# Two graph-attention layers on one core: another order of calls in the edge loop, a written order for its last steps, and no phase between the layers

## The chip, the core and the metric

The kernel runs on one core of a Trainium2 chip. Its engines work side by side and wait for each other through semaphores: PE (TensorE) multiplies and transposes, ACT (ScalarE) evaluates functions and copies, DVE (VectorE) works element by element, POOL (GpSimd) issues the indirect gathers, SP (SyncE) issues the plain DMAs. The metric is the device time of one execution in microseconds, as the median of the runs. Profiles come from one profiled execution; durations in this document are read from it.

## The reference

`x` has 3125 nodes of 128 features; 100,000 edges are given as `src` and `dst`, sorted by `dst`. Two layers (`DEPTH = 2`) with two heads each are computed, and the sum with the input is normalised:

```python
for i in range(DEPTH):
    h = _layer_norm(x, ln1_g[i], ln1_b[i])
    g = _gatv2(h, src, dst, Wl[i], bl[i], Wr[i], br[i], att[i], gat_b[i])
    x = x + (g @ proj_W[i] + proj_b[i])
    h = _layer_norm(x, ln2_g[i], ln2_b[i])
    x = x + (jax.nn.gelu(h @ W1[i] + b1[i]) @ W2[i] + b2[i])
# _gatv2: xl = h @ Wl + bl, xr = h @ Wr + br
#   score = einsum(leaky_relu(xl[src] + xr[dst]), att); alpha = segment softmax of score over dst
#   out = segment_sum(xl[src] * alpha, dst) + gat_b
# after the layers: x = _layernorm(x_in + x)
```

## The kernel before

**Tables.** A first phase (`setup`) builds index tables; a second (`project_nodes`) writes `xl` of layer 0 and its scores' linear part to a table in HBM, 130 numbers per node and head, and `xr` split into three bf16 parts. Between the layers stands one more phase, `begin_layer`, which copies the starting tables back (`reset_state` on POOL, `reset_tables` and `make_dests` on DVE).

**Edge loop.** The 100,000 edges are cut into 391 units of 256. A step handles two units, so there are 196 steps (`NO`), the last with one unit. Each unit takes two indirect gathers of 128 rows on POOL (L969, tile `rows`), 782 per layer. POOL may run ten steps ahead of the sums (`sums_ready`, L966). For step i the engines do:

- PE `project(u)` (L1091, L1094): transposes the gathered rows into PSUM and adds `xr`; ACT `relu` (L1209) reads it into `lz`.
- PE `score(i-1)` (L1066, L1071, L1077); ACT `keep_scores` (L1230) copies the scores out; DVE `lowest` (L1363 to L1382) finds each window's running extreme, one step after another, since `nm` is carried on; ACT `exponent` (L1222) makes the weights `ex`.
- PE `turn(i-4)` (L1143) transposes the weights, ACT `weigh` (L1215) copies them to `wgt`, PE `total(i-5)` (L1160) sums the rows by them, DVE `accumulate` (L1454) adds into `acc`.
- DVE `one_hot` (L1351) prepares the next step's masks, ACT `linear` (L1237) its linear part.

**Nodes.** When a tile of 128 nodes has all its edges, about every eighth step, it is carried through the rest of the layer, spread over some 20 steps by `nodes(i, at)`: ACT `stg` (L1303, L1306), PE L1109, DVE division (L1473), PE L1118, ACT `gT`, PE L1123, DVE `x1` and its moments, ACT square root, DVE `xn2`, PE L1168, ACT `h2`, PE L1129, ACT gelu (L1290), PE L1176, DVE `x2`, and in layer 0 the next layer's projection (L1135), split into three parts (L1507, L1563) and stored by SP (L1029, L1033, L1038); in layer 1 the normalised output (L1534, L1023). The last five tiles, 20 to 24, are called T0 to T4 here; T3 and T4 can only begin when the last steps' sums are in.

**What sets the order.** Every engine's program is written out by Python loops over i; nothing reorders it. In the loop of before PE calls `turn(i - 4)` first in a step, ahead of the projections (L1180 to L1190), and ACT calls `weigh` and `exponent` ahead of `keep_scores` and `linear` (L1316 to L1328). From step 195 another fixed order holds to the end (L1191, L1329), and after the last sums DVE also brings the tables of window positions on (`next_pass`, `next_tables`, L1389 to L1429).

## Time and profile before

| | us |
|---|---|
| median of 3 runs (lowest, highest) | 2196.34 (2195.72, 2197.27) |
| the profiled execution | 2195.76 |
| its span, first to last instruction | 2194.1 |
| gathers of layer 0, first start to last end | 92.68 to 1076.88 |
| gathers of layer 1, first start to last end | 1149.34 to 2131.37 |

The span is 1.66 us shorter than the profiled execution's own time, and that is 0.58 us below the median. Of the engines' busy shares PE has 78%, POOL 70%, ACT 67% and DVE 56%. These are averages over two long loops and the stretches behind them; which engine sets the pace has to be read from the waits. Idle time marked "issue" is time in which an engine waited for nothing that the profile shows.

### The profile page before, as it was taken

Reading aid. Unit: us, or ns where it says so; the run is one execution under the profiler, and the core shown is the slowest. Engines: PE = TensorE matmul, PEld = TensorE weight load, DVE = VectorE, ACT = ScalarE, POOL = GpSimd, SP = SyncE. Lnnn points to the kernel's source line nnn. Section 1 sums busy time; section 2 is a strip of 40 time slices with the busy share of each in tenths; the row PEclk is TensorE's granted clock in tenths of the full one; section 3 lists DMA queues with packets and bytes.
Section 4 is the critical chain, followed back from the end, with each engine's and each line's share of the span. In section 5 each row is a group of like instructions: output and inputs, shape, how many; then the busy total and the mean of one; then the engine's idle time right before and its main releaser. Section 6 shows DMA issues by size and latency. Waiting matters only on the chain. (4 is left out here: it accounts for less than half of the span.)

```text
span 2194.1 us, 67356 instructions
## 1 busy us (share of the span) xinstructions
PE 1706.7 (78%) x19783; PEld 1308.7 (60%) x19783; DVE 1233.8 (56%) x5168; ACT 1462.3 (67%) x3260; POOL 1541.2 (70%) x1664
## 2 busy tenths in 40 slices
PE   2677887888888888888846778888887888778885
PEld 1355666666666666666534556666666666666664
DVE  7545565556565565556553455554655555555554
ACT  4455777777777777677634567677777776677674
POOL 3777777777777777777407777777777777777760
PEclk6888998999999999999977988998999899999896
DMA  4655556666666666665316556556556565565540
GB/s 114 202 157 152 158 162 165 168 161 170 162 165 165 162 171 165 161 169 164 100 37 171 153 148 167 158 154 164 156 155 165 153 166 160 149 167 158 151 132 9
DMA packets 236751, 332.74 MB, mean 152 GB/s; under 512 B 51010, under 2 KB 160490, under 8 KB 236394
## 3 DMA queue, kind: packets, MB, share of 16 engines
q0 software_dynamic: 75072, 208.30, 36.8%
q1 hardware_dynamic: 161322, 120.16, 18.5%
q8 instruction: 165, 2.70, 0.5%
q14 instruction: 192, 1.57, 0.2%
HBM read 308.02 MB, written 20.25 MB: 150 GB/s over the span
## 5 line engine op out<-in xcount | busy, mean ns | idle before, releaser
L969 POOL DMA_INDIRECT rows<-table,src_t x1564 | 1490.3, 953 | 483.7 <-issue 468.3
L1209 ACT ACTIVATE lz<-psum 128x512 f32<-128x512 f32 x782 | 467.0, 597 | 550.0 <-PE psum L1094 530.0
L1091 PE MATMUL psum<-ident,rows 128*128 128x128 f32 x3128 | 536.3, 299 | 111.5 <-DMA rows<-table,src_t 111.0
L1454 DVE SCALAR_TENSOR_TENSOR acc<-acc,keep,psum 128x129 f32 x782 | 273.0, 349 | 602.1 <-PE psum L1160 348.2
L1091 PEld LDWEIGHTS psum<-ident,rows 128*128 128x128 f32 x3128 | 409.8, 155 | 148.4 <-DMA rows<-table,src_t 139.3
L1143 PE MATMUL psum<-ident,ex 128*128 128x128 f32 x784 | 175.7, 308 | 292.6 <-ACT ex L1222 289.6
L1094 PE MATMUL psum<-oh,xrw 96*128 96x256 bf16 x1564 | 332.9, 297 | 0.0
L1143 PEld LDWEIGHTS psum<-ident,ex 128*128 128x128 f32 x784 | 87.3, 147 | 379.2 <-ACT ex L1222 347.7
L1160 PE MATMUL psum<-rows,wgt 128*32 128x129 f32 x6256 | 255.7, 285 | 5.3 <-DVE acc L1454 4.7
L1077 PE MATMUL psum<-lz,att_w 128*32 128x256 f32 x3128 | 257.2, 407 | 0.0
L1364 DVE TENSOR_REDUCE low<-hold_s 128x1 f32<-128x256 f32 x392 | 161.9, 413 | 164.1 <-ACT hold_s L1230 162.6
L1160 PEld LDWEIGHTS psum<-rows,wgt 128*32 128x32 f32 x6256 | 186.2, 116 | 103.2 <-issue 35.7
L1222 ACT ACTIVATE ex<-hold_s,peak 128x256 f32<-128x256 f32 x392 | 201.9, 515 | 66.7 <-DVE peak L1382 63.2
L1351 DVE TENSOR_SCALAR oh<-relb,win_col,less 128x256 bf16<-128x256 int16 x782 | 234.9, 344 | 11.1 <-DMA relb<-cyc_d 10.9
L1094 PEld LDWEIGHTS psum<-oh,xrw 96*128 96x128 bf16 x1564 | 167.9, 107 | 15.9
L1066 PE MATMUL psum<-ident,lin 128*128 128x128 f32 (+1 forms) x784 | 164.6, 294 | 0.0
L1237 ACT COPY lin<-rows 128x256 f32<-128x256 f32 x392 | 161.9, 413 | 0.0
L1230 ACT COPY hold_s<-psum 128x256 f32<-128x256 f32 x392 | 142.6, 364 | 17.5 <-PE psum L1077 17.1
L1215 ACT COPY wgt<-psum 128x256 f32<-128x256 f32 x392 | 143.6, 366 | 0.9 <-PE psum L1143 0.9
L1109 PE MATMUL psum<-stg,sel 128*64 128x129 f32 x1200 | 117.9, 291 | 4.3 <-ACT stg L1306 4.3
L1071 PE MATMUL psum<-oh,mask_w 128*32 128x256 bf16 x1564 | 120.6, 298 | 0.0
L1222 ACT ACT_TABLE_LOAD x90 | 115.5, 1283 | 1.6
(245 smaller groups left out, 1970.3 us busy)
## 6 DMA issues: line engine op xcount, KB each, us to landing
xrw<-xr_split SPq DMA_DIRECT2D x782, 48.0 KB
relb<-rel_d SPq DMA_DIRECT2D x194, 192.0 KB
rows<-table,src_t POOLq DMA_INDIRECT x1564
relb<-cyc_d SPq DMA_DIRECT2D x194, 64.0 KB
xr_split<-split SPq DMA_DIRECT2D x50, 192.0 KB, 1.9
table<-row SPq DMA_DIRECT2D x50, 130.0 KB, 2.1
x_mid<-x SPq DMA_DIRECT2D x25, 64.0 KB
xo<-x_mid SPq DMA_DIRECT2D x25, 64.0 KB
```

The lines of the kernel that those rows point to most:

```text
L969: pool.indirect_dma_start(rows[:, ring(u), t, u % M, :, :].rearrange("p h c -> p (h c)"), None, s["tables"][layer][0:NP, :], bass.Indirect ...
L1066: pe.matmul(out[0:n, t * P:t * P + P], lin[:, g % 2, t, 0:n], s["ident"][:, :], is_transpose=True, start=(t == 0), stop=False, skip_group_ ...
L1077: m = pe.matmul(out[o:o + W, 0:UE], w["att_w"][:, h * W:h * W + W], lz[:, u % (2 * M), h * UE:h * UE + UE], start=False, stop=True, skip_g ...
L1091: pe.matmul(z[:, o:o + P], rows[:, ring(u), t, u % M, h, 0:D], s["ident"][:, :], is_transpose=True, start=(h == 0 and t == 0), stop=False, ...
L1094: m = pe.matmul(z[:, h * UE:h * UE + UE], xrw[:, place(u), h * D:h * D + D], oh[0:3 * W, u % (3 * M), :], start=False, stop=(h == H - 1), ...
L1143: m = pe.transpose(ps[4][:, t * P:t * P + P], ex[:, g % 2, t * P:t * P + P], s["ident"][:, :])
L1160: m = pe.matmul(sum_bank(g)[o:o + W, c:c + D + 1], wgt[:, g % 2, t, q:q + W], rows[:, ring(u), t, u % M, h, 0:D + 1], start=True, stop=True)
L1209: act.activation(lz[:, u % (2 * M), :], ps[u % M][:, :], ACT.Relu).then_inc(lz_ready, 1)
L1222: act.activation(ex[0:n, g % 2, :], hold_s[0:n, c, :], ACT.Exp, bias=peak[0:n, c:c + 1], scale=-1.0).then_inc(ex_ready, 1)
L1237: act.copy(lin[:, g % 2, :, :].rearrange("p t (c w) -> p (t c) w", w=W), rows[:, ring(g * M), :, :, :, D + 1:RC].rearrange("p t u h c -> p ...
L1351: m = v.tensor_scalar(oh[:, u % (3 * M), :], relb[:, u % RING, :], s["win_col"][:, 0:1], s["less"][:, 0:1], ALU.is_equal, ALU.subtract)
L1454: m = v.scalar_tensor_tensor(a, a, s["keep"][:, u:u + 1], sum_bank(g)[:, c:c + D + 1], ALU.mult, ALU.add)
```

## The change

**Edge loop.** On PE `turn(i - 4)` moves behind `project` and `score`, ahead of `total(i - 5)`. On ACT `keep_scores` and `linear` come ahead of `weigh` and `exponent`. The loops end at step 190 (`DRAIN = NO - 6`); DVE loads some slot numbers earlier so that the last steps need no loads.

**Last steps.** From there on each engine has a written list of calls. In it T3 and T4 have buffers of their own (`slot`, four each for `x2`, `xn1`, `row`, `xrf`, `rest`, `split`), T2 to T4 have a second PSUM bank (`alt`), the next projection is cut into a right and a left half, and SP loads the stores' places before it waits for data.

**Layers.** `begin_layer` is gone. The tables are brought on, or set back at a layer's end, by POOL behind its last gather (`next_places`, `restart_places`, `next_window`, `restart_window`, `next_tables`), and POOL takes three each of the additions `xob` and `x1b` for T2 to T4. The places of both layers' stores are prepared in `project_nodes` (one `make_dests` more on DVE).

The diff, cut to its core (the functions named in the lists hold the same instructions as before unless said above):

```diff
         for layer in range(L):
-            if layer > 0:
-                scratch(begin_layer, st, layer)
             with nc.Fori(0, n_pass) as _:
                 scratch(edge_pass, wts, st, layer)
...
-def begin_layer(nc, sb, sem, ps, s, layer):
-
-    state = sem("state")
-    moved = sem("moved")
-    with nc.Block() as block:
-        @block.gpsimd
-        def _(pool):
...
+    def next_places(pool):
+
+        link(pool, pool.tensor_scalar(s["count"][:, :], s["count"][:, :], 1.0, None, ALU.add))
+        link(pool, pool.tensor_tensor(hop[:, :], s["at_s"][:, :], s["at_a"][:, :], ALU.subtract))
+        link(pool, pool.tensor_tensor(hop[:, :], hop[:, :], s["at_a"][:, :], ALU.subtract))
+        link(pool, pool.tensor_scalar(hop[:, :], hop[:, :], float(TRASH), s["gen"][0:1, :], ALU.add, ALU.mult))
+        link(pool, pool.tensor_tensor(s["at_a"][:, :], s["at_a"][:, :], hop[:, :], ALU.add))
...
+    def restart_places(pool):
+
+        link(pool, pool.tensor_scalar(over[:, :], s["gen"][:, :], -8.0 * NT, s["count"][:, 0:1], ALU.mult, ALU.add))
+        link(pool, pool.tensor_scalar(over[:, :], over[:, :], 0.5, None, ALU.is_ge))
...
+    T0, T1, T2, T3, T4 = range(NT - 5, NT)
+    DRAIN = NO - 6
+    assert node_step(T0) + 16 == node_step(T1) + 8 == node_step(T2) == DRAIN + 4 and (NU - 3) % RELS == 0
...
+            bias_residual(T2)
+            next_places(pool)
+            bias_residual(T3)
+            if not last:
+                restart_places(pool)
+            bias_residual(T4)
+            pool.wait_ge(added, NO)
+            next_window(pool)
+            if not last:
+                restart_window(pool)
+            bias_middle(T2)
+            next_tables(pool)
+            bias_middle(T3)
+            bias_middle(T4)
+            pool.wait_ge(staged, NT)
+            link(pool, pool.tensor_copy(s["tab_s"][:, :], tf[:, :]))
+            if not last:
+                link(pool, pool.tensor_scalar(s["acc"][:, 0, :], s["acc"][:, 0, :], on[:, 0:1], None, ALU.mult))
+            tables_moved = make_dests(pool, s, layer, moved, moves[0])
+            pool.wait_ge(listed, 1)
+            set_dests(pool, s, layer, moved, tables_moved)
+
...
+                        store_split(t, place_of(t))
+            rels(NU - 3)
+            ranges(NO - 4)
+            if last:
+                store_out(T0, places_of(T0))
+            ranges(NO - 3)
+            old_rows(T2)
+            if not last:
+                store_row(T0, place_of(T0))
+            ranges(NO - 2)
+            ranges(NO - 1)
...
+                store_split(T0, place_of(T0))
+                old_rows(T3)
+                to1, to2, to3, to4 = [place_of(t) for t in (T1, T2, T3, T4)]
+                sp.sem_inc(listed)
+                store_middle(T1, to1)
+                old_rows(T4)
+                store_middle(T2, to2)
+                store_middle(T3, to3)
+                store_middle(T4, to4)
+                store_row(T1, to1)
+                store_row(T2, to2)
+                store_row(T3, to3)
+                store_split(T1, to1)
+                store_split(T2, to2)
+                store_row(T4, to4)
+                store_split(T3, to3)
+                store_split(T4, to4)
...
-            for i in range(NO - 1):
-                if of_step(i - 4):
-                    turn(i - 4)
-                late_work(i)
-                for u in of_step(i):
-                    project(u)
-                if of_step(i - 1):
-                    score(i - 1)
...
+            for i in range(DRAIN):
                 for u in of_step(i):
                     project(u)
                 if of_step(i - 1):
@@ -1197,8 +1384,111 @@
                     turn(i - 4)
                 if of_step(i - 5):
                     total(i - 5)
...
+            score(NO - 7)
+            turn(NO - 10)
...
+            project(NU - 1)
+            score(NO - 2)
+            score(NO - 1)
+            turn(NO - 4)
+            total(NO - 5)
+            total(NO - 4)
+            project_sums(T2)
+            turn(NO - 3)
+            total(NO - 3)
+            turn(NO - 2)
+            total(NO - 2)
+            turn(NO - 1)
+            total(NO - 1)
+            combine(T3, 0)
+            combine(T3, 1)
+            combine(T4, 0)
+            combine(T4, 1)
+            turn_sums(T3)
+            narrow(T1)
+            turn_sums(T4)
+            project_sums(T3)
+            project_sums(T4)
+            turn_second(T2)
+            widen(T2)
+            turn_second(T3)
+            turn_second(T4)
...
+                turn_first(T4)
+                project_right(T4)
+                project_left(T4)
...
-            for i in range(NO - 1):
-                early_nodes(i)
+                    bias_sums(t)
                 for u in of_step(i):
                     relu(u)
-                if of_step(i - 4):
-                    weigh(i - 4)
-                middle_nodes(i)
-                if of_step(i - 3):
-                    exponent(i - 3)
                 if of_step(i - 1):
                     keep_scores(i - 1)
                 linear(i)
-                late_nodes(i)
-            for i in range(NO - 1, END):
-                for u in of_step(i):
-                    relu(u)
-                if of_step(i):
-                    linear(i)
-                if of_step(i - 1):
-                    keep_scores(i - 1)
+                if of_step(i - 4):
+                    weigh(i - 4)
...
+            exponent(NO - 1)
+            weigh(NO - 2)
+            weigh(NO - 1)
+            act.activation(spare[:, 0:1], s["eps_t"][:, 0:1], ACT.Gelu_apprx_tanh)
+            stage(T3, at_T3)
+            stage(T4, at_T4)
+            gelu(T1)
+            act.activation(spare[:, 1:2], s["eps_t"][:, 0:1], ACT.Sqrt)
+            bias_sums(T3)
+            deviation2(T2)
+            bias_sums(T4)
+            deviation1(T1)
+            deviation2(T3)
+            scale_second(T2)
+            deviation2(T4)
+            act.activation(spare[:, 2:3], s["eps_t"][:, 0:1], ACT.Gelu_apprx_tanh)
+            gelu(T2)
+            scale_second(T3)
...
+            gelu(T3)
+            gelu(T4)
+            act.activation(spare[:, 3:4], s["eps_t"][:, 0:1], ACT.Sqrt)
+            deviation1(T2)
...
+            for i in range(DRAIN):
+                accumulate(i - 6)
...
+            accumulate(NO - 7)
+            divide_sums(T2)
+            next_hot(NO - 1)
+            lowest(NO - 4)
+            accumulate(NO - 6)
+            lowest(NO - 3)
+            lowest(NO - 2)
+            accumulate(NO - 5)
+            lowest(NO - 1)
+            accumulate(NO - 4)
+            add_first(T2)
+            accumulate(NO - 3)
+            moments_second(T2)
+            accumulate(NO - 2)
+            accumulate(NO - 1)
+            divide_sums(T3)
+            divide_sums(T4)
+            add_second(T1)
+            moments_first(T1)
...
+                remainder(T4)
+                add_left(T4)
+                third_part(T3)
+                third_part(T4)
```

**PE, a step of layer 0's loop, before:** `ident,rows` and `oh,xrw` are the projections of two units, `ident,lin` to `lz,att_w` the score, `ident,ex` the turn, `rows,wgt` the sum.

```order
L1143 MATMUL psum<-ident,ex 128x128 x2
L1091 MATMUL psum<-ident,rows 128x128 x4
L1094 MATMUL psum<-oh,xrw 128x256 x2
L1091 MATMUL psum<-ident,rows 128x128 x4
L1094 MATMUL psum<-oh,xrw 128x256 x2
L1066 MATMUL psum<-ident,lin 128x128 x2
L1071 MATMUL psum<-oh,mask_w 32x256 x4
L1077 MATMUL psum<-lz,att_w 32x256 x4
L1160 MATMUL psum<-rows,wgt 32x129 x8
```

The same step in the changed kernel:

```order
L1275 MATMUL psum<-ident,rows 128x128 x4
L1278 MATMUL psum<-oh,xrw 128x256 x2
L1275 MATMUL psum<-ident,rows 128x128 x4
L1278 MATMUL psum<-oh,xrw 128x256 x2
L1250 MATMUL psum<-ident,lin 128x128 x2
L1255 MATMUL psum<-oh,mask_w 32x256 x4
L1261 MATMUL psum<-lz,att_w 32x256 x4
L1287 MATMUL psum<-ident,ex 128x128 x2
L1304 MATMUL psum<-rows,wgt 32x129 x8
```

The turn stood first in the step; it now stands eighth, between the score and the sum.

**PE, the last turns and sums of layer 0, before** (`ident,xn`, `h,w` and `wlr,h` are node work of T1 and T0, `stg,sel` the gathering of a tile's sums from the staged windows):

```order
L1143 MATMUL psum<-ident,ex 128x128 x2
L1160 MATMUL psum<-rows,wgt 32x129 x8
L1143 MATMUL psum<-ident,ex 128x128 x2
L1160 MATMUL psum<-rows,wgt 32x129 x8
L1143 MATMUL psum<-ident,ex 128x128 x2
L1160 MATMUL psum<-rows,wgt 32x129 x8
L1168 MATMUL psum<-ident,xn_3 128x128
L1172 MATMUL psum<-ident,xn_3 128x128
L1160 MATMUL psum<-rows,wgt 32x129 x4
L1129 MATMUL psum<-h_3,w_0 128x128 x4
L1135 MATMUL psum<-wlr,h_3 128x512
L1109 MATMUL psum<-stg_3,sel 64x129 x6
```

The same in the changed kernel (`pw,gT` projects T2's sums, `an` are the divided sums of T3 and T4, `w_0,ge` the second half of T1's hidden layer):

```order
L1304 MATMUL psum<-rows,wgt 32x129 x16
L1337 MATMUL psum<-pw,gT_3 128x128 x2
L1287 MATMUL psum<-ident,ex 128x128 x2
L1304 MATMUL psum<-rows,wgt 32x129 x8
L1287 MATMUL psum<-ident,ex 128x128 x2
L1304 MATMUL psum<-rows,wgt 32x129 x8
L1287 MATMUL psum<-ident,ex 128x128 x2
L1304 MATMUL psum<-rows,wgt 32x129 x4
L1319 MATMUL psum<-stg_3,sel 64x129 x24
L1330 MATMUL psum<-ident,an_3 128x128 x2
L1358 MATMUL psum<-w_0,ge_3 128x128 x4
L1330 MATMUL psum<-ident,an_3 128x128 x2
```

Before the last sum (x4) came transposes of T1 and T0, and a hidden layer and a projection stood between it and the first half of T3's gathering (x6). Now that sum follows its turn, and all four halves for T3 and T4 (x24) follow it at once.

**POOL, from the last gathers of layer 0 to those of layer 1, before:**

```order
L969 DMA rows<-table,src_t 128x260 x782
L959 UNCONDITIONAL_BRANCH
L128 ISA
L179 REGISTER_ALU
L179 COMPARE_AND_BRANCH
L732 UNCONDITIONAL_BRANCH
L707 MEMSET step 128x1
L708 MEMSET count 1x1
L709 COPY win_col<-win_col 128x1
L710 COPY at_x<-at_x 1x391
L711 COPY at_s<-at_s 1x391
L712 COPY at_a<-at_a 1x391
```

In the changed kernel POOL goes on behind the gathers, within the same phase (the first 11 of 50 instructions):

```order
L1033 DMA rows<-table,src_t 128x260 x782
L1045 TENSOR_TENSOR xob_3<-xo_3,pb_row 128x128
L964 TENSOR_SCALAR count<-count 128x1
L965 TENSOR_TENSOR hop<-at_s,at_a 1x391
L966 TENSOR_TENSOR hop<-hop,at_a 1x391
L967 TENSOR_SCALAR hop<-hop,gen 1x391
L968 TENSOR_TENSOR at_a<-at_a,hop 1x391
L969 TENSOR_SCALAR at_x<-at_x,step 1x391
L972 TENSOR_SCALAR at_s<-at_s,step 1x391
L973 TENSOR_SCALAR hop<-at_s 1x391
L974 TENSOR_TENSOR at_s<-at_s,hop 1x391
L1045 TENSOR_TENSOR xob_3<-xo_3,pb_row 128x128
```

The copies of a phase of its own became arithmetic on the tables behind the last gather.

## Rows read from the trace of the kernel before

**Rows 1.** The page, part 1: busy time, share of the span, instructions

```profile
PE 1706.7 (78%) x19783; PEld 1308.7 (60%) x19783; DVE 1233.8 (56%) x5168; ACT 1462.3 (67%) x3260; POOL 1541.2 (70%) x1664
```

**Rows 2.** Line 969, POOL's gathers: ns min/median/max; idle before them until

```profile
L969 POOL DMA_INDIRECT rows<-table,src_t x1564: 940/946/1291, 92.7 to 2130.4; - x196
...
  issue: 468.3, 1525
  PE psum L1160: 11.0, 36
```

**Rows 3.** POOL in order of time: start us, us, what, idle before it

```profile
92.68 1.18 POOL L969 DMA_INDIRECT rows<-table,src_t  x1 [3.97 <-issue]
...
1075.94 0.94 POOL L969 DMA_INDIRECT rows<-table,src_t  x1 [0.30 <-issue]
1143.55 0.10 POOL L707 MEMSET step<- 128x1 f32 x1 [66.67 <-SPq L731]
...
1149.34 0.97 POOL L969 DMA_INDIRECT rows<-table,src_t  x1 [3.73 <-POOLq L129]
...
2130.42 0.95 POOL L969 DMA_INDIRECT rows<-table,src_t  x1 [0.30 <-issue]
```

**Rows 4.** PE's waits: us in total, times, longest us

```profile
PE psum L1143 <- ACT ex L1222: 289.6, 171, 3.1
PE psum L1091 <- DMA rows<-table,src_t: 111.0, 70, 17.7
```

**Rows 5.** POOL, then PE, in order of time, about us 2028

```profile
2026.97 0.95 POOL L969 DMA_INDIRECT rows<-table,src_t  x1 [0.30 <-issue]
...
2029.74 0.66 PE L1091 MATMUL psum<-ident,rows 128*128 128x128 f32 x4 [1.02 <-DMA rows<-table,src_t]
```

**Rows 6.** PE in order of time, at the end of layer 0

```profile
1073.00 0.38 PE L1143 MATMUL psum<-ident,ex 128*128 128x128 f32 x2
...
1075.94 1.16 PE L1109 MATMUL psum<-stg,sel 128*64 128x129 f32 x12
1079.92 0.44 PE L1143 MATMUL psum<-ident,ex 128*128 128x128 f32 x2 [2.82 <-ACT ex L1222]
...
1084.90 0.66 PE L1091 MATMUL psum<-ident,rows 128*128 128x128 f32 x4
...
1108.95 4.18 PE L1109 MATMUL psum<-stg,sel 128*64 128x129 f32 x36 [0.58 <-ACT stg L1306]
```

**Rows 7.** The page, part 5: one costly group

```profile
L1209 ACT ACTIVATE lz<-psum 128x512 f32<-128x512 f32 x782 | 467.0, 597 | 550.0 <-PE psum L1094 530.0
```

**Rows 8.** DVE in order of time, at both layers' ends

```profile
1089.28 0.42 DVE L1364 TENSOR_REDUCE low<-hold_s 128x1 f32<-128x256 f32 x1 [0.66 <-ACT hold_s L1230]
...
1090.59 0.83 DVE L1454 SCALAR_TENSOR_TENSOR acc<-acc,keep,psum 128x129 f32 x2
...
1102.35 0.35 DVE L1454 SCALAR_TENSOR_TENSOR acc<-acc,keep,psum 128x129 f32 x1 [0.48 <-DVE acc L1454]
...
1137.99 0.76 DVE L1563 TENSOR_TENSOR split<-rest,split 128x256 bf16<-128x256 f32 x2
...
2156.60 0.35 DVE L1454 SCALAR_TENSOR_TENSOR acc<-acc,keep,psum 128x129 f32 x1 [0.48 <-DVE acc L1454]
```

**Rows 9.** ACT, then SP, in order of time, at both layers' ends

```profile
1107.66 1.03 ACT L1303 COPY stg<-acc 128x1032 f32 x1
...
2178.09 1.14 ACT L1290 ACTIVATE ge<-psum,b_col 128x128 f32<-128x128 f32 x4 [0.17 <-PE psum L1129]
...
2189.49 0.26 SPq L1023 DMA_DIRECT2D out_dram<-xn  x1
```

**Rows 10.** A window of layer 1's end: us, busy by engine, PEclk, DMA

```profile
2157.00:2179.40 22.40, 15.74 (x95) 13.56 (x96) 10.83 (x44) 12.54 (x30) 0.00 (x0) 0.69 0.04 11
```

**Rows 11.** DVE in order of time, while POOL was busy

```profile
87.50 0.59 DVE L749 TENSOR_SCALAR valid<-valid 1x25 f32<-1x25 f32 x1
...
88.78 0.17 DVE L757 TENSOR_TENSOR dest<-dest,valid 1x25 f32<-1x25 f32 x1
```

999 lines of the change are left out of this document (639 added, 360 removed).

## The prediction

> **What bounds the kernel now.** I read five views, in this order. The page's first part [rows 1] shows no engine above 78% busy, so it does not name a bound. The view of the gathers' line does [rows 2]: 1564 gathers of 0.95 us, and the idle time before 1525 of them is 468.3 us, 0.31 us each, released by nothing but POOL's own issue. Only 36 waited for the sums, 11.0 us in all, which is the same 0.3 us each. POOL in order of time says the same [rows 3]: layer 0's gathers run from 92.68 to 1076.88, 984.2 us for 782, or 1.26 us each; layer 1's from 1149.34 to 2131.37, 982.0 us. The reader is to see that POOL never waits for the other engines in these 1966 us, so that they all follow at 5.03 us a step (four gathers). What PE waits for [rows 4] is then read rightly: it loses 289.6 us in 171 waits for the exponentials, and it still comes back to waiting for gathered rows 70 times, 111.0 us. In the loop PE's waits are slack.
>
> Outside the gathers lie 92.7 us ahead, 66.7 us between a last gather and `begin_layer` [rows 3], 5.8 us more to the next gather, and 62.7 us behind the last. These 135 us behind gathers are bound by chains, and there each wait counts. Their marks: rows land 1.8 us after POOL is done with a gather (2027.92 to 2029.74, [rows 5]), so unit 390 of layer 0 could be projected at 1078.7; PE begins it at 1084.90 [rows 6], since it had stood 2.82 us before a turn while ACT served a node's gelu, and three steps' work was in line. The last `accumulate` ends at 1102.70 and in layer 1 at 2156.95 [rows 8]; then T3 and T4 go through the whole node chain, 40.9 us to 1143.55 and 37.2 us to 2194.1.
>
> **The change part by part.**
>
> *The turn in the loop.* It removes PE's 289.6 us of waits for the exponentials: with projections and score (2.3 of a step's 2.94 us, 1073.00 to 1075.94, [rows 6]) ahead of it, the exponential has that much longer. But POOL sets the step. What is late next is the gathered row: PE will wait for it instead. I cost it at nothing; the cover is POOL's 1.26 us a gather. Bounds: a gain of at most the 11.0 us in [rows 2], and a loss only if the new order makes PE or ACT slower than 5.03 us a step (a rival below). ACT's new order puts `keep_scores` behind a wait for the score; behind it stand `linear`, `weigh` and `exponent`, for which PE waits one step later, so nobody waits now. DVE's extra loads of slots in some 20 steps fall into its 44% idle time [rows 1]. What the new order does give is that PE is not behind at the end: I take the last projection at data arrival, 1078.7 in layer 0 and 2133.2 in layer 1 (2131.37 + 1.8).
>
> *From the last projection to the last `accumulate`.* The written lists leave no node work there but T2's sums. The chain: projection and score of step 194 1.6 us, copy 0.4, `lowest` 1.3 (1089.28 to 1090.59, [rows 8]), `accumulate` 0.8 (same row), the last `lowest` 1.2, two exponentials 0.95, `weigh` 0.35, sum 0.65, turn 0.4, `weigh` 0.35, the last sum 0.45, the last `accumulate` 0.45, and 0.7 for eleven hand-overs: 9.6 us. The PE parts are shares of the 2.94 us step; none of the ACT parts is longer than the 0.60 us of the costliest one [rows 7]. Before took 17.8 us (1084.90 to 1102.70). So the bounds are 9.6 and 17.8; I take 10.6, near the lower, with 1.0 us for a slow clock and for POOL, which now works beside DVE. Ends: 1089.3 and 2143.8. Against 1102.70 and 2156.95 that is 13.4 and 13.2 us less.
>
> *From there to the end of the layer.* Before, staging T3, a gelu between two table loads and staging T4 took 6.3 us until PE could begin the last three of the four gatherings (1102.70 to 1108.95, [rows 6, 8]). Now one table load, begun before the last `accumulate`, and two stagings of 1.29 us (1107.66 to 1108.95, [rows 6, 9]) take 3.1 us; but PE has four gatherings left instead of three, 1.4 us each (4.18 for three, [rows 6]). Net 1.8 us. Behind them the lists bring T2, T3 and T4 through together; what a missing wait between them gives I put at 1.2 us (bounds: 4 us lost, 5 won; the tiles wait on ACT for the gelu table as before). In layer 0 the end is then DVE's row of 14 additions, as before (1137.99, [rows 8]), and 4.8 us to the next phase. In layer 1 the places of the stores are loaded ahead. Between the last gelu (2179.23) and the last store (2189.49) lie 10.3 us [rows 9] with four such loads on the way; I take 3 us for them (bounds 0 and 4). Sum: 3.0 us less in layer 0, 6.0 in layer 1.
>
> *No phase between layers.* From 1143.55 to 1149.34 are 5.8 us [rows 3]; a phase needs some time from its barrier to its first gather even so, and I keep 0.9 of it (bounds 0 and 1.8): 4.9 us less. POOL's work that replaces it, 50 small instructions, begins behind the rows' arrival and is covered by the some 45 us that the node chains still need; what it can cost is a rival.
>
> *Setup.* DVE gets 12 small operations for the second layer's places, 0.17 us to 0.59 us each [rows 11], 2 to 7 us. DVE had been done some 3 us before the first gather; I take 0.5 us (bounds 0 and 4).
>
> Sum: 13.4 + 13.2 + 3.0 + 6.0 + 4.9 − 0.5 = 40.0 us. The profiled execution took 2195.76 us, 0.6 below the median of 2196.34: 2155.8, and by the median 2156.3. I predict 2156 us.
>
> **The rivals.**
>
> *POOL and SP hold T4 and T2 back.* In layer 0 SP issues `old_rows(T4)` only behind `store_middle(T1)`, and POOL stands at `bias_residual(T4)` until it lands; queued behind it are `next_window`, `restart_window` and `bias_middle` of T2 to T4, for which DVE's second additions wait. `store_middle(T1)` comes about 9.5 us after the last sum and the load some 3 us later, which my order of DVE's calls meets with 1.3 us of waiting; if the some 20 linked operations behind it take 0.3 us longer each, `add_second(T2)` and its followers are late by 6. And DVE is slower beside POOL: with POOL busy an operation of 25 elements took 0.59 us, a like one 0.17 with POOL done [rows 11]. With 10 such meetings in each tail that is 8.4 us. Together, at half of each 7 to 14: 2168 us. Against it: `low`, `nm` and `peak` are tiny, and much of DVE's work reads PSUM.
> The Trainium skill (SBUF — State Buffer, "SBUF: two separate sides") states a rule that speaks against the change: VectorE and GpSimd share one port pair as an exclusive lock, held for a whole instruction. By that rule the trace's 0.59 against 0.17 us is expected, and each meeting would cost up to the rest of a POOL instruction.
>
> *Only half of the gain between projection and last sum.* `nm` is carried from step to step, each sum of the last five waits for `acc`, and the clock may fall: in the window behind the sums it is 0.69 of full speed [rows 10], nearer the lower of its two levels, 1.2 GHz, than 2.4. If PE's parts take 1.7 times as long and its waits remain, each tail saves 6.7 us instead of 13.3: 2169 us.
>
> *The lists do nothing.* If each tail ends with a chain as long as before and only the phase goes: 2196.3 − 4.4 = 2192 us. For it speaks that the four table loads and DVE's 14 last additions stay.
>
> *Slower.* The loop is no longer POOL's. Place: ACT at a node's gelu, where two table loads and four functions come behind `weigh` and ahead of `exponent`; the turn, the sum and by `sums_ready` the gathers of ten steps later wait for it. It decides from the point where a round of eight steps costs PE or ACT more than 40.2 us. PE has 111.0 us of waits for rows over 49 rounds, 2.3 us a round [rows 4], in hand, beside what it lost to exponentials. If a round grew by 2 us beyond that, 48 rounds would cost 96 us: 2196 − 40 + 96 = 2252 us. Against it: the turn has more time than before, and `linear`, on which the next score hangs, now comes before the gelu.
>
> **How the numbers follow.** The forecast has 0.61, POOL and SP 0.16, half the gain 0.12, the lists without effect 0.05, slower 0.04, and 0.02 remains for no change. The range goes from 2146 (the sum with the better bounds of the middle terms, 10 us more saved) to 2173, beyond the two rivals at 2168 and 2169; outside lie the last three cases and a tenth of the others. A change of 0.2% (4.4 us) is about what a measurement of this kernel can tell from none. The case of 2192 is at that edge and counts as faster by half: faster 0.92, same 0.04, slower 0.04.
>
> **What would show it.** The gathers should again run 982 to 985 us per layer, with nothing but issue before them; a wait for the sums there would be the slower rival. The exponentials' row among PE's waits should fall from 289.6 to under 100 us, and that for gathered rows rise by about as much. The last projection should begin within 1 us of 1.8 us after the last gather, and the last `accumulate` end 10 to 12 us after it. The first gather of layer 1 should start at about 1128.5, some 51 us behind the end of the last of layer 0 instead of 72.5, and from the end of the last gather of layer 1 to that of the span should be about 43.5 us instead of 62.7. If DVE's small operations beside POOL's tables are above 0.3 us, or DVE waits for `x1b` from POOL, the first rival holds. The forecast is wrong if these two stretches shrink by less than 12 us each.

## The result

| | us |
|---|---|
| the kernel before, same chip, 4 runs | 2196.07 (2195.72 to 2197.27) |
| the changed kernel, 4 runs | 2177.67 (2176.00 to 2178.62) |
| ratio, 95% interval | 0.9915 (0.9901 to 0.9929) |
| predicted | 2156 (2146 to 2173) |

The change makes the kernel 18.4 us faster. I had predicted 40 us, and the range does not hold the time. The profiled execution took 2176.0 us with a span of 2174.3; the sum of the prediction would have made that span 2154.1. So 20.2 us are missing. Marks in the two profiles, at which the span is cut into stretches, say where:

| us | before | predicted | after |
|---|---|---|---|
| first gather | 92.7 | 93.2 | 93.3 |
| layer 0, first to last gather | 984.2 | 984.2 | 982.3 |
| last gather to last `accumulate` | 25.8 | 12.4 | 18.9 |
| from there to layer 1's first gather | 46.6 | 38.7 | 43.6 |
| layer 1, first to last gather | 982.0 | 982.0 | 981.9 |
| last gather to last `accumulate` | 25.6 | 12.4 | 20.4 |
| from there to the end of the span | 37.2 | 31.2 | 33.9 |

The marks are POOL's and DVE's rows in the changed kernel (here of layer 0):

```profile
1074.61 0.95 POOL L1033 DMA_INDIRECT rows<-table,src_t  x1 [0.30 <-issue]
...
1138.10 1.10 POOL L1033 DMA_INDIRECT rows<-table,src_t  x1 [17.09 <-issue]
```

```profile
1094.11 0.35 DVE L1794 SCALAR_TENSOR_TENSOR acc<-acc,keep,psum 128x129 f32 x1 [0.42 <-PE psum L1304]
```

The loops are as predicted. 14.5 us are missing between the last gather and the last sum, 4.9 behind it in layer 0, 2.7 in layer 1; 2.0 came back in the loops.

### The profile page after: what moved, and what is told of

It is laid out like the page before. It is cut to its first block and busy times, and to the rows that moved or that the text cites. A ratio compares the mean times of both kernels' runs of the same rounds, so it can differ in the third digit from the quotient of the medians.

```text
span 2174.3 us, 67462 instructions
## 1 busy us (share of the span) xinstructions
PE 1764.8 (81%) x19833; PEld 1221.8 (56%) x19833; DVE 1223.9 (56%) x5104; ACT 1469.3 (68%) x3260; POOL 1590.1 (73%) x1749
## 3 DMA queue, kind: packets, MB, share of 16 engines
q1 hardware_dynamic: 161322, 120.16, 18.4%
## 5 line engine op out<-in xcount | busy, mean ns | idle before, releaser
L1499 ACT ACTIVATE lz<-psum 128x512 f32<-128x512 f32 x782 | 455.2, 594 | 428.6 <-PE psum L1278 411.2
L1275 PE MATMUL psum<-ident,rows 128*128 128x128 f32 x3128 | 516.8, 290 | 263.1 <-DMA rows<-table,src_t 186.2
L1275 PEld LDWEIGHTS psum<-ident,rows 128*128 128x128 f32 x3128 | 364.9, 147 | 371.1 <-DMA rows<-table,src_t 248.4
L1278 PE MATMUL psum<-oh,xrw 96*128 96x256 bf16 x1564 | 315.5, 284 | 0.0
L1304 PE MATMUL psum<-rows,wgt 128*32 128x129 f32 x6256 | 264.1, 288 | 17.7 <-DVE acc L1794 14.8
L1736 DVE TENSOR_SCALAR oh<-relb,win_col,less 128x256 bf16<-128x256 int16 x782 | 237.7, 348 | 14.8 <-DMA relb<-cyc_d 11.5
L1512 ACT ACTIVATE ex<-hold_s,peak 128x256 f32<-128x256 f32 x392 | 201.9, 515 | 30.1 <-DVE peak L1767 27.1
L1287 PE MATMUL psum<-ident,ex 128*128 128x128 f32 x784 | 180.0, 313 | 49.1 <-ACT ex L1512 48.6
L1287 PEld LDWEIGHTS psum<-ident,ex 128*128 128x128 f32 x784 | 82.1, 146 | 226.3 <-issue 142.3
L1304 PEld LDWEIGHTS psum<-rows,wgt 128*32 128x32 f32 x6256 | 154.8, 112 | 92.1 <-issue 86.0
L1278 PEld LDWEIGHTS psum<-oh,xrw 96*128 96x128 bf16 x1564 | 160.3, 103 | 12.0
L1505 ACT COPY wgt<-psum 128x256 f32<-128x256 f32 x392 | 148.2, 378 | 6.9 <-PE psum L1287 6.2
```

The source lines that it names most:

```text
L1275: pe.matmul(z[:, o:o + P], rows[:, ring(u), t, u % M, h, 0:D], s["ident"][:, :], is_transpose=True, start=(h == 0 and t == 0), stop=False, ...
L1278: m = pe.matmul(z[:, h * UE:h * UE + UE], xrw[:, place(u), h * D:h * D + D], oh[0:3 * W, u % (3 * M), :], start=False, stop=(h == H - 1), ...
L1287: m = pe.transpose(ps[4][:, t * P:t * P + P], ex[:, g % 2, t * P:t * P + P], s["ident"][:, :])
L1304: m = pe.matmul(sum_bank(g)[o:o + W, c:c + D + 1], wgt[:, g % 2, t, q:q + W], rows[:, ring(u), t, u % M, h, 0:D + 1], start=True, stop=True)
L1499: act.activation(lz[:, u % (2 * M), :], ps[u % M][:, :], ACT.Relu).then_inc(lz_ready, 1)
L1512: act.activation(ex[0:n, g % 2, :], hold_s[0:n, c, :], ACT.Exp, bias=peak[0:n, c:c + 1], scale=-1.0).then_inc(ex_ready, 1)
```

## The profile after

The gathers' line and PE's waits, to be read against [rows 2, 4] (engine, what it waited for, us in total, times, longest):

```profile
L1033 POOL DMA_INDIRECT rows<-table,src_t x1564: 942/946/1287, 93.3 to 2119.1; - x196
  issue: 487.2, 1530
  PE psum L1304: 8.5, 28
```

```profile
PE psum L1275 <- DMA rows<-table,src_t: 186.2, 144, 15.3
PE psum L1275 <- DVE oh L1736: 73.2, 94, 1.4
PE psum L1287 <- ACT ex L1512: 48.6, 56, 1.2
```

POOL still waits for nothing but its own issue (the 28 waits for PE are 0.3 us each, as long as its own issue). The wait for the exponentials fell from 289.6 to 48.6 us, and PE waits for rows and for `one_hot` (`oh`) instead: in the loop, where POOL sets the pace, PE still has time to spare.

PE and ACT in order of time, where the written lists of layer 0 begin (start, duration, idle time and its releaser; PE's last row is the last projection of layer 1):

```profile
1054.86 0.44 PE L1287 MATMUL psum<-ident,ex 128*128 128x128 f32 x2
1059.82 0.47 PE L1365 MATMUL psum<-ident,xn 128*128 128x128 f32 x1 [4.52 <-DVE xn L1878]
...
1061.89 1.09 PE L1304 MATMUL psum<-rows,wgt 128*32 128x129 f32 x16 [1.39 <-DVE acc L1794]
...
1065.21 0.80 PE L1275 MATMUL psum<-ident,rows 128*128 128x128 f32 x4
...
1084.35 0.60 PE L1275 MATMUL psum<-ident,rows 128*128 128x128 f32 x4
...
2130.09 0.60 PE L1275 MATMUL psum<-ident,rows 128*128 128x128 f32 x4
```

```profile
1057.33 1.28 ACT L1559 ACT_TABLE_LOAD   x1 [2.75 <-issue]
```

The list starts with node work of T0 and T1. ACT stands 2.75 us in six register loads of slot numbers, then loads a table; PE stands 4.52 us for that and 1.39 us for `accumulate`, and only then projects the units of step 190 (1065.21). From there to unit 390 (1084.35) it is busy nearly all the time, 19.1 us for five steps, 3.8 us a step against the gatherings' 5.03, with two of T2's gatherings (1.15 us each) and T1's widening (1.16 us) in the list. So it regains about 6 us and still projects unit 390 8.8 us behind the last gather (1075.56), where the prediction had 1.8. In layer 1 it is 10.1 us (2120.02 to 2130.09). In the kernel before the same distances were 8.0 (1076.88 to 1084.90) and 7.6 us: the last projection did not come sooner behind the gathers, but later.

DVE and POOL there (`nxt` and `peak` are the last operations of `lowest`):

```profile
1079.72 0.21 DVE L1756 TENSOR_TENSOR_SCAN nm<-fresh,nm,low 64x2 f32<-64x2 f32 x1
1079.97 0.93 DVE L1759 TENSOR_TENSOR nxt<-nm,fresh 64x2 f32<-64x2 f32 x1
1080.93 0.15 DVE L1766 TENSOR_TENSOR peak<-nxt,nm 64x1 f32<-64x1 f32 x1
1081.10 0.88 DVE L1767 TENSOR_TENSOR peak<-nxt,nm 64x1 f32<-64x1 f32 x1
```

```profile
1079.87 1.01 POOL L965 TENSOR_TENSOR hop<-at_s,at_a 1x391 f32<-1x391 f32 x1
1080.96 1.01 POOL L966 TENSOR_TENSOR hop<-hop,at_a 1x391 f32<-1x391 f32 x1
1082.08 0.61 POOL L967 TENSOR_SCALAR hop<-hop,gen 1x391 f32<-1x391 f32 x1
...
1086.97 1.58 POOL L973 TENSOR_SCALAR hop<-at_s 1x391 f32<-1x391 f32 x1
```

```profile
1088.05 0.15 DVE L1766 TENSOR_TENSOR peak<-nxt,nm 64x1 f32<-64x1 f32 x1
```

`nxt` and `peak` take 0.15 us and the scan 0.21, except where they meet an operation of POOL. Beside a `TENSOR_TENSOR` DVE's end falls with POOL's (1080.88, 1081.97). Beside a `TENSOR_SCALAR` of over 1 us only those that begin near its start are late: during L973 (1086.97 to 1088.55) scan, `nxt` and both `peak` took their 0.21 and 0.15 us.

The end of layer 0, DVE, POOL, SP and PE:

```profile
1103.45 0.28 DVE L1825 TENSOR_TENSOR x<-psum,xob 128x128 f32<-128x128 f32 x1
...
1111.51 0.29 DVE L1825 TENSOR_TENSOR x<-psum,xob 128x128 f32<-128x128 f32 x1 [7.23 <-POOL x1b L1059]
```

```profile
1106.32 0.45 POOL L1045 TENSOR_TENSOR xob<-xo,pb_row 128x128 f32<-128x128 f32 x1 [3.87 <-DMA xo<-in_x_dram]
1106.88 0.27 POOL L988 TENSOR_SCALAR win_col<-step,win_col 128x1 f32<-128x1 f32 x1
...
1110.92 0.45 POOL L1059 TENSOR_TENSOR x1b<-x,b_row 128x128 f32<-128x128 f32 x1
```

```profile
1102.73 0.35 SPq L1141 DMA_DIRECT2D x_mid<-x  x1
1103.13 0.32 SPq L1109 DMA_DIRECT2D xo<-in_x_dram  x1
```

```profile
1112.84 0.95 PE L1344 MATMUL psum<-ident,xn 128*128 128x128 f32 x2 [6.67 <-DVE xn L1841]
...
1116.63 3.62 PE L1351 MATMUL psum<-h,w 128*128 128x128 f32 x16
```

This is the queue that the first rival described: SP issues `old_rows(T4)` only behind `store_middle(T1)` (1102.73), POOL stands 3.87 us for it, then eleven linked small operations (1106.88 to 1110.92) stand ahead of the `x1b` of T2 whose end the buffer of `x1(T4)` waits for. DVE stands 7.23 us ahead of the first addition of T4; the rival had named the second additions, which stand behind it. The first gather of layer 1 starts at 1138.10.

The end of layer 1, SP's stores of the output (two windows of one view):

```profile
2163.96 1.66 SPq L1135 DMA_DIRECT2D out_dram<-xn  x2
```

```profile
2169.11 0.23 SPq L1135 DMA_DIRECT2D out_dram<-xn  x1
```

T4's store waits until T3's have landed (the kernel asks for it), 3.5 us after their issue (2165.62 to 2169.11), and the span ends 5.0 us behind the end of its issue.

## The experiments

The first four ran on one chip, on which the kernel before took 2195.27 us; the changed kernel was not run there again. I held that PE is late because of the head of its list (theory A), against a chain that makes up for it anyway (rival B).

**e_slots**

```diff
+                if DRAIN - 6 <= i < DRAIN - 3:
+                    t = T2 + i - (DRAIN - 6)
+                    ahead[t] = slots_of(t)
...
-            at_T2, at_T3, at_T4 = slots_of(T2), slots_of(T3), slots_of(T4)
+            at_T2, at_T3, at_T4 = [ahead[t] for t in (T2, T3, T4)]
```

> The changed kernel, but ACT's six loads of slot numbers for staging T2 to T4, which stand at the head of its written list (2.75 us without work in each layer ahead of the square root's table load), are made in the loop six, five and four steps ahead of its end. Theory A (PE comes late to the last projections because the written lists begin with node work behind ACT's loads: it projects the units of step 190 some 10 us after their rows landed and, being busy 3.8 us a step against 5.03 of the gatherings, regains only part): PE's wait of 4.5 us for the normalised rows there falls by 2.7, the last projection and the last accumulate come 2.0 to 2.8 us earlier in each layer, and the time falls by 4 to 5.6 us to 2172 to 2174 from 2177.7. Rival B (the pace of the last steps is set by the running extreme and the exponentials, so that a later or earlier start is evened out before the last sum): under 1 us.

Measured: 2174.99 us (2172.64 to 2177.49), 0.9905 (0.9888 to 0.9921). ACT's 2.75 us became 0.47 and PE's wait 2.12:

```profile
1055.83 1.28 ACT L1559 ACT_TABLE_LOAD   x1 [0.47 <-DVE moments L1836]
```

```profile
1058.31 0.33 PE L1365 MATMUL psum<-ident,xn 128*128 128x128 f32 x1 [2.12 <-DVE xn L1882]
```

The units of step 190 were projected 2.3 us sooner behind the gathers, unit 390 1.1 and 0.8 us sooner (7.7 and 9.3), and the last `accumulate` came 19.5 and 21.0 us behind the last gather instead of 18.9 and 20.4. The stop shrank, but the last sum did not come sooner. The median is 2.7 us below the changed kernel's; the runs of the two overlap.

**e_front**

```diff
             score(NO - 7)
+            project(NU - 11)
+            project(NU - 10)
             turn(NO - 10)
...
             weigh(NO - 10)
+            relu(NU - 11)
+            relu(NU - 10)
```

> The changed kernel, but the two projections of step 190 stand at the head of PE's written list (ahead of the turn, the two transposes of node tiles and a sum that wait for ACT and DVE), and their two relu on ACT ahead of scale_first(T0). Theory A: 1.6 us of PE's work move into its 5.9 us of idle time, the last projection comes 1.0 to 1.6 us earlier in each layer, 2174.5 to 2176. Rival B: no difference, within 1 us. A third outcome, slower by 1 to 2 us, if the two relu delay the table load chain more than PE gains.

Measured: 2176.7 us (2175.42 to 2179.88), 0.9918 (0.9901 to 0.9934), no difference. The last projection came 7.7 and 7.8 us behind the last gather, the last `accumulate` 20.4 and 18.9. Of the four ends of e_slots and e_front, in all of which the last projection came 0.8 to 2.3 us sooner, three have the last sum 0.6 to 1.5 us later and one 1.5 us sooner. That does not bear out theory A as I put it. How well such a mark repeats is seen in e_mid, which has the same instructions up to there and shows 20.5 and 21.5 us: 1.1 to 1.6 us more than the changed kernel's.

What took the gain back can be read from the last 5 us before the last sum, here of layer 0 of the changed kernel and of e_front (us, busy times of PE, PEld, DVE, ACT, POOL, granted clock PEclk, DMA share, GB/s):

```profile
1089.46:1094.46 5.00, 2.53 (x44) 1.31 (x44) 3.90 (x14) 2.99 (x6) 4.46 (x8) 1.00 0.00 0
```

```profile
1093.14:1098.14 5.00, 3.06 (x28) 1.37 (x28) 2.83 (x10) 2.81 (x5) 4.47 (x6) 0.51 0.02 3
```

The granted clock there was 1.00 in both layers of the changed kernel, 0.81 and 0.56 in e_slots, 0.51 and 0.79 in e_front, 1.00 and 0.55 in e_mid. In e_front's layer 0 PE had stood 1.14 us for an exponential before; then the sixteen-part sum took 1.09 us instead of 0.65 and the turn 0.69 instead of 0.44. From the last projection to the last sum it took 10.1 and 10.3 us in the changed kernel, 11.8 and 11.7 in e_slots, 12.7 and 11.1 in e_front. Whether the sooner projection brings the lower clock with it, no run separates.

**e_mid**

```diff
-                store_middle(T1, to1)
                 old_rows(T4)
+                store_middle(T1, to1)
...
             bias_residual(T4)
+            bias_middle(T2)
             pool.wait_ge(added, NO)
             next_window(pool)
             if not last:
                 restart_window(pool)
-            bias_middle(T2)
```

> The changed kernel, but in layer 0 SP issues old_rows(T4) ahead of store_middle(T1), and POOL does bias_middle(T2) directly behind bias_residual(T4), ahead of next_window and restart_window. Theory C (DVE's 7.2 us of waiting ahead of x1(T4) in layer 0 is the load queued behind a store and 4.2 us of linked small POOL operations ahead of the x1b that its buffer waits for): that wait falls under 1 us and the time by 5.5 to 7 us, to 2171 to 2172. Rival: the chain behind is bound elsewhere (PE at its lower clock, SP's stores of the middle rows), so that the end of layer 0 moves by less than 3 us. Layer 1 should not move by more than 0.5 us in either.

Measured: 2168.5 us (2165.97 to 2172.24), 0.9879 (0.9863 to 0.9896). The stretch from the last `accumulate` to layer 1's first gather fell from 43.6 to 34.1 us, 9.5 us and so more than the wait of 7.2. The median is 9.2 us below the changed kernel's, more than the 5.5 to 7 expected. Most of the rest is PE's clock. Windows of PE work behind the wait, of the changed kernel and of e_mid:

```profile
1112.00:1122.00 10.00, 8.64 (x42) 7.74 (x43) 2.65 (x13) 7.42 (x19) 5.31 (x15) 0.59 0.03 8
```

```profile
1106.00:1112.00 6.00, 4.24 (x34) 3.58 (x33) 3.38 (x15) 4.92 (x14) 4.79 (x14) 1.00 0.04 11
```

and the same sixteen matmuls, 3.62 us above, in e_mid:

```profile
1110.87 1.95 PE L1351 MATMUL psum<-h,w 128*128 128x128 f32 x16
```

After standing 6.67 us PE worked at 0.59 of full speed, near the lower of its two levels (1.2 of 2.4 GHz); without the wait at full speed, and the sixteen matmuls took 1.7 us less. The Trainium skill ("TensorE: Matmul & The Clock Gate", Part 1) says that the array's clock is at the lower level when it has been idle; the trace agrees.

**e_loop** (the kernel before with only the loop's new order)

```diff
             for i in range(NO - 1):
-                if of_step(i - 4):
-                    turn(i - 4)
                 late_work(i)
...
                     score(i - 1)
+                if of_step(i - 4):
+                    turn(i - 4)
```

(ACT likewise: `keep_scores` and `linear` ahead of `weigh` and `exponent`.)

> The kernel before with nothing but the new order in the loop: PE's turn behind projections and score, ACT's keep_scores and linear ahead of weigh and exponent, up to step 194; its end, its phase between layers and its tables as before. What the prediction claimed (the new order leaves PE in time at the end): the last projection within 1 us of its rows instead of 6 us late, and some 5 us less in each layer, 2186. Theory A (late at the end because of the table loads and node work in the last steps, which the order doesn't remove): 0 to 2 us per layer, 2192 to 2196. In both PE's wait for exponentials falls from 290 us to under 60 and the gatherings take 982 to 984 us a layer as before.

Measured: 2187.44 us (2186.04 to 2188.54), 0.9964 (0.995 to 0.9978). PE's wait for the exponentials is gone; two waits for node work took its place:

```profile
PE psum L1091 <- DMA rows<-table,src_t: 156.6, 126, 17.8
PE psum L1168 <- DVE xn L1521: 105.4, 48, 2.5
PE psum L1176 <- ACT ge L1290: 69.4, 47, 1.5
```

The last projection came 7.8 us behind the last gather in layer 0 (before: 8.0) and 5.2 in layer 1 (7.6). So the order alone does not bring PE to data arrival, though the time is near what I expected for that case (2186) and not what theory A gave. By the medians it gives 7.8 us: 4.9 in the two stretches behind the gathers (71.8 for 72.5 us, 58.4 for 62.7), and 3.6 in the loops, where the 1564 gathers took 1486.6 us instead of 1490.3, 2.4 ns less each. Why they are shorter stays open.

**All further kernels** ran on four other chips, here called B to E, where the kernel before took 2752.8, 2697.7, 2699.1 and 2700.5 us (labels f_, g_, h_, j_). POOL's gathers are as long there, but it waits for the sums. The gathers' line of h_mid:

```profile
L1033 POOL DMA_INDIRECT rows<-table,src_t x1564: 943/949/1258, 93.3 to 2609.2; - x196
  issue: 381.6, 1184
  remote: 305.6, 209
  PE psum L1304: 278.0, 164
```

```profile
PE psum L1287 <- issue: 116.9, 61, 3.1
PE psum L1275 <- issue: 115.3, 170, 9.0
```

PE stands there without a releaser that the trace shows (the two longest rows of h_mid are above), a step takes 6.2 to 6.3 us, and the last projection comes 16.6 to 21.4 us behind the last gather. Kernels are compared on one chip only.

All of these kernels are e_mid with further edits; h_mid is e_mid itself. **f_tables, g_tables, h_tables** leave POOL's operations on the 391-wide tables out (with these inputs their result isn't needed):

```diff
     def next_places(pool):
         link(pool, pool.tensor_scalar(s["count"][:, :], s["count"][:, :], 1.0, None, ALU.add))
-        link(pool, pool.tensor_tensor(hop[:, :], s["at_s"][:, :], s["at_a"][:, :], ALU.subtract))
...
-        for to, of in ((s["at_x"], s["at_x0"]), (s["at_s"], s["at_s0"]), (s["at_a"], s["at_a0"])):
...
```

**f_late, g_late, h_late, j_late** move T2's and T1's node work behind the last projection (ACT's `bias_sums(T2)`, DVE's `divide_sums`, `add_first` and `moments_second` of T2 follow):

```diff
-            combine(T2, 0)
             score(NO - 5)
...
             total(NO - 4)
-            project_sums(T2)
+            widen(T1)
             turn(NO - 3)
+            combine(T2, 0)
             total(NO - 3)
+            combine(T2, 1)
             turn(NO - 2)
```

**f_all, g_all**: e_slots, e_front, and in layer 1

```diff
-                store_out(T1, to1)
                 first_rows(T4)
+                store_out(T1, to1)
                 store_out(T2, to2)
-                store_out(T3, to3)
```

with T3's three stores issued by ACT. **f_both, g_both, h_both, j_both**: f_all and f_late together.

> The kernel of e_mid (2168.5) with POOL's operations on the 391-wide position tables left out behind the last gather (eight of next_places, nine of restart_places); with these inputs they would move the tables and set them back, so the result doesn't need them. Theory P (DVE's scan, nxt and peak, which took up to 0.93 us beside such an operation against 0.15 to 0.21 alone, lie on the chain to the last accumulate): all of them fall back to 0.15 to 0.21, the last accumulate comes 1.5 to 2.5 us sooner behind the last projection in each layer, 2163.5 to 2165.5. Rival (the long ones fall into DVE's waits): within 1 us of 2168.5.

> The kernel of e_mid with T2's gatherings (two of 1.15 us), its transposes and T1's widening (1.16 us) taken out of PE's list ahead of the last projection and put between and behind the last turns and sums, where PE waited; T2's division, bias and first addition follow them on DVE and ACT. Theory D (PE is never idle from step 191 on, so each us of node work in its list makes the last projection late): the last projection 3 to 3.8 us sooner (6 us instead of 9.6 behind the last gather), the last accumulate 2 to 3.5 us sooner, 2162 to 2165. Rival (the last sums hang on the running extreme and the exponentials, and the work moved lands between them): no gain or up to 2 us lost, 2168 to 2171.

> e_mid with the edits of e_slots and e_front, and in layer 1 SP's load of x0(T4) ahead of store_out(T1), and the three stores of T3's rows on ACT's queue instead of SP's. If the gains add up: 2.7 (e_slots), 1.0 (e_front), 0.5 for x0 and 1.5 for the stores, which land sooner, so that T4's store behind them starts sooner: 2162.5 to 2164.5. If the first two only shorten a wait that the chain to the last sum makes anyway, only the last two count: 2166 to 2167.

> All edits of f_all and f_late together. With theory D and the gains of f_all: 2157 to 2161. If the last accumulate doesn't follow the last projection: 2165 to 2168.

> f_tables again, since its call ran on a chip on which the kernel before, too, took 2752.8 us: e_mid (2168.5) without POOL's operations on the 391-wide tables behind the last gather. Theory P: scan, nxt and peak at 0.15 to 0.21 us, the last accumulate 9.8 to 10.2 us behind the last projection (there 9.8 against 11.5 to 11.9 of the other three) instead of 10.9 and 11.9, 2164.5 to 2166.5. Rival: within 1 us of 2168.5.

> f_late again: e_mid with T2's gatherings and T1's widening behind the last projection. Theory D: last projection 3 to 3.8 us sooner than e_mid's 9.6, last accumulate 2 to 3.5 us sooner than its 20.5 and 21.5 behind the last gather, 2162 to 2165. Rival: no gain or up to 2 us lost, 2168 to 2171.

> f_all again: e_mid with the edits of e_slots and e_front, x0(T4) ahead of store_out(T1) and T3's stores on ACT's queue. Additive: 2162.5 to 2164.5; if slots and front only shorten a wait that the chain makes anyway: 2166 to 2167.

> f_both again: all edits of f_all and f_late. With theory D 2157 to 2161; if the last accumulate doesn't follow the last projection 2165 to 2168.

> e_mid once more, as the base of this call: 2168.5 where the kernel before takes 2195; its last accumulate 20 to 21.5 us behind the last gather in both layers.

> e_mid without POOL's operations on the 391-wide tables behind the last gather. Theory P: last accumulate 9.8 us behind the last projection (in the two calls before always 9.8, against 10.9 to 11.9 with the tables), 1.5 to 2 us less per layer, 3 to 4 us less than h_mid in all. Rival: the sooner projection-to-sum chain is taken back behind it, within 1 us of h_mid.

> e_mid with T2's gatherings and T1's widening behind the last projection. Theory D: last accumulate 2 to 3.5 us sooner behind the last gather than in h_mid, 4 to 6 us less in all. Rival (chain-bound): within 1 us of h_mid or up to 2 us more.

> e_mid with slots, front, late, x0(T4) sooner and T3's stores on ACT's queue: 6 to 9 us less than h_mid if theory D holds and the rest adds 2 to 3; 1 to 3 less if only the stores count.

> e_mid with T2's gatherings and T1's widening behind the last projection. On a chip where the kernel before takes about 2195: theory D 0.9850 of it (6 us less than e_mid's 0.9879), last projection 6 us and last accumulate 17.5 us behind the last gather; rival 0.9875 to 0.9890, last accumulate still at 20 to 21.5. Where it takes about 2700: 2 us less than e_mid would, as in the last call.

> All the edits together (e_mid, slots, front, late, x0(T4) sooner, T3's stores on ACT's queue). On a chip where the kernel before takes about 2195: theory D 2155 to 2160; rival 2163 to 2167. Where it takes about 2700: 0.9876 of it, as in the last call.

Measured, each against the kernel before on the same chip; in brackets the last `accumulate` behind the last gather, layers 0 and 1:

| | chip B (f_) | C (g_) | D (h_) | E (j_) |
|---|---|---|---|---|
| mid | | | 2674.21, 0.9908 (0.9890 to 0.9926) [33.2, 31.0] | |
| tables | 2709.01, 0.9832 (0.9805 to 0.9860) [29.2, 29.1] | 2670.36, 0.9896 (0.9879 to 0.9913) [29.8, 29.5] | 2671.03, 0.9897 (0.9879 to 0.9916) [29.8, 28.8] | |
| late | 2710.43, 0.9832 (0.9804 to 0.9860) [29.2, 28.1] | 2673.23, 0.9903 (0.9885 to 0.9922) [30.8, 29.9] | 2672.27, 0.9907 (0.9889 to 0.9926) [29.2, 29.5] | 2672.76, 0.9894 (0.9877 to 0.9911) [30.8, 29.4] |
| all | 2705.74, 0.9814 (0.9786 to 0.9842) [31.4, 31.0] | 2669.48, 0.9891 (0.9872 to 0.9910) [31.4, 30.1] | | |
| both | 2704.01, 0.9816 (0.9788 to 0.9844) [29.2, 30.4] | 2663.69, 0.9873 (0.9856 to 0.9889) [30.8, 30.2] | 2663.93, 0.9876 (0.9855 to 0.9898) [30.8, 28.2] | 2668.39, 0.9876 (0.9859 to 0.9893) [30.2, 30.1] |

- *Tables.* Without POOL's operations no scan, `nxt` or `peak` of DVE behind the last gather was over its 0.15 to 0.21 us in either layer of g_tables and h_tables. With them they lost 2.1 and 1.4 us in the changed kernel, 1.8 and 1.5 in e_mid, 2.2 and 0.8 in h_mid (sums of what exceeds 0.21 for the scan, 0.15 for the others). h_tables, DVE:

```profile
1337.41 0.21 DVE L1743 TENSOR_TENSOR_SCAN nm<-fresh,nm,low 64x2 f32<-64x2 f32 x1
1337.66 0.15 DVE L1746 TENSOR_TENSOR nxt<-nm,fresh 64x2 f32<-64x2 f32 x1
1337.85 0.15 DVE L1753 TENSOR_TENSOR peak<-nxt,nm 64x1 f32<-64x1 f32 x1
```

  So the delay is shown to come from POOL's operations. How much of it lies on the way to the last sum is less. DVE waits 2.1 to 2.5 us for the scores of step 194 (`hold_s`) in each of these ends, and what it lost before that falls into the wait. Behind the wait it lost 0.3 and 0.5 us in the changed kernel, 1.1 and 0.9 in e_mid, 1.1 and 0.0 in h_mid. From the last projection to the last `accumulate` it took 9.8 us in all six ends of f_tables, g_tables and h_tables; with the operations it took 11.8 and 9.8 us in h_mid, 10.1 and 9.8 in f_all and in g_all. Of the 3.4 and 2.2 us by which h_tables' last `accumulate` came sooner than h_mid's only 2.0 and 0.0 lie in that stretch; the rest is a last projection that came 1.4 and 2.2 us sooner. My expectations for g_tables and h_tables ("9.8 against 11.5 to 11.9 of the other three") overlooked f_all and g_all. The median is 3.2 us lower, as expected (3 to 4), but the runs overlap (2668.11 to 2674.13, 2671.10 to 2676.30): an effect on the time is not shown.
- *Late.* The last projection came 17.7 and 18.0 us behind the last gather instead of h_mid's 21.4 and 21.2, so 3.7 and 3.2 us sooner, as theory D said (3 to 3.8). Over chips B to E it is 16.6 to 19.3 us in the eight ends of the late kernels and 19.0 to 21.4 in the eight ends of mid and tables, which have PE's list of e_mid: the node work in that list does make the last projection late, by how much is less sure. The last `accumulate` came at 29.2 and 29.5 instead of 33.2 and 31.0. From the last projection to it 11.5 us passed in every end of the late and both kernels, against 9.8 in the tables kernels: T2's gatherings, now between the last turns, cost part of the gain there. The median fell by 1.9 us, within the spread: less than the 4 to 6 expected. On a chip where the kernel before takes about 2195 us this was not measured.
- *Both.* h_both's runs (2662.89 to 2667.25) lie below all of h_mid's, 10.3 us by the medians, more than expected. In its profile 7.1 of 12.7 us lie in the stretches behind the gathers, 5.8 in the loops, which I can't explain. T3's stores on ACT gave nothing: from the first of T2's stores to T4's it took as long as before, since T4's waits for T3's landing on either queue (SP in e_mid and in j_both):

```profile
2154.09 7.12 SPq L1135 DMA_DIRECT2D out_dram<-xn  x7
```

```profile
2655.37 7.34 SPq L1135 DMA_DIRECT2D out_dram<-xn  x4
```

The version to hand on is both (f_both), by these four chips; where the kernel before takes about 2195 us, e_mid was the fastest measured, 2168.5 us, some 8 us under the changed kernel by the two ratios to before, and both was not measured.

## Why the prediction was wrong

1. **Loop bound by POOL, new order costs nothing there**: right. 982.3 and 981.9 us, nothing but issue ahead of the gathers.
2. **"What the new order does give is that PE is not behind at the end: I take the last projection at data arrival"**: this step failed. The last projection came 8.8 and 10.1 us behind the last gather instead of 1.8, 15.3 of the missing 20.2 us. I read PE's lateness of before off one wait (2.82 us for a gelu, [rows 6]) and took its removal for the removal of the lateness. But PE is late because the last steps hold more than the loop's: node work of T0 to T2, and a stop of 5.9 us where the written lists begin, on ACT's register loads, table load and DVE's sums. e_loop shows that the order alone leaves 7.8 and 5.2 us, h_late, on chip D, that T2's gatherings and T1's widening in the list were worth 3.7 and 3.2 us of lateness in one pair of profiles. With the stop cut by 2.2 us in e_slots the last projection came 1.1 and 0.8 us sooner, and still the last sum did not: the stretch behind grew, with the clock and DVE's late operations in it. How much sooner the last sum would come with a punctual projection stays open; what the changed kernel did gain in this part (6.9 and 5.2 us sooner last sums) came from the next term alone.
3. **From the last projection to the last `accumulate` 10.6 us**: right, 10.1 and 10.3 (before 17.8 and 18.0). The 9.6 us of the chain were near the 9.8 of the six ends without POOL's table operations, and DVE beside POOL added 0.3 and 0.5 us. That the 1.0 us for the clock and POOL was enough was partly luck: the clock stayed at 1.00 there, and in the ends of e_slots, e_front and e_mid the same stretch took 10.9 to 12.7 us. Had the projection been punctual, the term could have been too small by up to 2 us (an estimate from these ends).
4. **From there to the end of the layer**: in layer 0 from the last `accumulate` to DVE's last addition it took 37.8 us (1094.46 to 1132.27) where before took 36.0 (1102.70 to 1138.74, [rows 8]) and I had 33.0. The first rival's place and queue were right (what waited was T4's first addition), and I gave it 0.16: the loss is 7.2 us of waiting and 2.3 more, 1.7 of them seen as slow clock, that I hadn't counted. e_mid gives 9.5 back, so without the wait the term would have been a gain of 7.7 instead of 3.0. In layer 1 the time to the last gelu fell by 3.0 us (22.3 to 19.3) as summed (1.8 + 1.2), but the 3 us for the stores' places came to 0.4 (14.9 us to 14.5 from the last gelu to the end): T4's store waits for T3's to land, so its place was loaded in time anyway.
5. **No phase**: right. From DVE's last addition to the first gather 5.8 us instead of 10.6, 4.8 less (predicted 4.9).
6. **Setup**: 0.6 us (predicted 0.5).

The range failed with the term of point 2 and the wait of point 4: its upper end allowed for one loss of 12 to 13 us, and the change met 14.5 us in one place and 4.9 in another. My own sign said it: the two stretches behind the gathers took 62.5 and 54.3 us instead of 51 and 43.5 and shrank by 9.9 and 8.5 us, less than the 12 each that I had asked for.

## What to carry to other kernels

When an engine is late at the end of a loop, add up its work over the last steps against the pace of arrival; removing the one wait seen there doesn't make it punctual. Before work is put on a queue as "covered", follow the first instruction behind it that another engine waits for: a load behind a store, an addition behind eleven linked small operations. A wait on the end's chain can cost more than its length where PE's clock falls during it (here 6.67 us of waiting, and 1.7 us more in the sixteen matmuls behind).
